# First attention layer: bank of the last first-score, place of the residual addition, and the order of the weight preparation

## The reference, cut to what matters

```python
x = _layernorm(x + attn0(x))   # 16 heads of 8, rotary positions, softmax(q k^T / sqrt(8)) v, then w_out and b_out
x = _layernorm(x + ffn0(x))    # ternary W_fc, gelu, layer norm with ln_w, ln_b, ternary W_proj
x = _layernorm(x + attn1(x))   # q = k, 16 heads mixed by W_x (16x16), then W_out
x = _layernorm(x + ffn1(x))    # silu(gate) * up, then down; int32 weights divided by 127
```

## Time and profile before

| | us |
|---|---|
| median of 3 runs | 1529.43 (1526.62 to 1534.0) |
| profiled run | 1530.18 |
| span from first to last instruction | 1527.9 |
| mean granted TensorE clock | 0.976 of full |
| TensorE busy / VectorE / ScalarE / GpSimd | 95% / 77% / 69% / 63% of the span |

### The profile page before, as it was taken

How to read it: one execution, slowest core, us unless ns; L and a number is a source line. 1 busy time by engine, 2 the same in 40 slices (tenths; PEclk the granted TensorE clock), 3 DMA queues, 4 the chain that set the end, 5 groups by cost and what they waited for, 6 DMA issues and landing times. The chain is left out here.

```text
span 1527.9 us, 55309 instructions
## 1 busy us (share of the span) xinstructions
PE 1456.4 (95%) x17642; PEld 1141.6 (75%) x17642; DVE 1180.8 (77%) x3338; ACT 1056.9 (69%) x2581; POOL 967.4 (63%) x1160
## 2 busy tenths in 40 slices
PE   5999999999999899979999999999999999998998
PEld 3445555554554499959989999999999999897997
DVE  4688888888888478878887888788878887864666
ACT  2477777777778888856777777777777777773332
POOL 4465565656554167777777877787778777852222
PEclk7699999999999999979999999999999999999999
DMA  5345454454444100122222222222222222201211
GB/s 146 105 128 135 132 140 128 132 140 126 134 131 135 34 32 33 55 74 79 82 69 90 76 79 69 90 76 80 69 90 76 80 70 85 75 23 32 65 62 52
DMA packets 174124, 133.93 MB, mean 88 GB/s; under 512 B 13787, under 2 KB 145126, under 8 KB 174054
## 3 DMA queue, kind: packets, MB, share of 16 engines
q1 hardware_dynamic: 172944, 132.37, 30.0%
q10 hardware_dynamic: 1110, 0.66, 0.1%
HBM read 64.82 MB, written 55.05 MB: 78 GB/s over the span
## 5 line engine op out<-in xcount | busy, mean ns | idle before, releaser
L971 DVE TENSOR_REDUCE shifts<-bank 128x2 bf16<-128x512 f32 x1024 | 682.2, 686 | 158.7 <-PE bank L1123 158.1
L912 ACT ACTIVATE probs<-bank 128x512 f32<-128x512 f32 x1024 | 579.9, 595 | 120.1 <-PE bank L1109 116.3
L1071 PE MATMUL bank<-values,probs 64*128 64x129 f32 x8192 | 577.8, 276 | 0.9 <-DVE o_even L938 0.7
L1071 PEld LDWEIGHTS bank<-values,probs 64*128 64x128 f32 x8192 | 528.8, 188 | 20.4 <-issue 4.5
L1123 PE MATMUL bank<-stack 48*128 48x256 bf16 x2048 | 373.3, 277 | 29.7 <-DVE shifts L971 24.1
L1109 PE MATMUL bank<-stack 49*128 49x256 bf16 x2048 | 373.3, 274 | 7.6 <-ACT probs L912 2.4
L715 POOL TENSOR_TENSOR values<-mix,v_in 128x1024 f32<-128x1024 f32 x128 | 302.3, 2363 | 0.0
L1109 PEld LDWEIGHTS bank<-stack 49*128 49x128 bf16 x2048 | 163.9, 95 | 139.4 <-ACT probs L912 89.7
L724 POOL TENSOR_TENSOR o_odd<-o_odd,scaled 128x256 f32<-128x256 f32 x224 | 163.5, 730 | 128.0 <-ACT scaled L838 124.3
L838 ACT ACTIVATE scaled<-bank,recips 128x128 f32<-128x128 f32 x448 | 138.6, 360 | 92.8 <-DVE recips L965 92.7
L1123 PEld LDWEIGHTS bank<-stack 48*128 48x128 bf16 x2048 | 156.2, 96 | 54.0 <-DVE shifts L971 37.8
(11 more groups left out here) (165 smaller groups left out, 2176.8 us busy)
## 6 DMA issues: line engine op xcount, KB each, us to landing
stack<-score_parts SPq DMA_DIRECT2D x64, 512.0 KB, 4.2
stack<-score_parts SPq DMA_DIRECT2D x256, 96.0 KB
score_parts<-parts SPq DMA_DIRECT2D x256, 64.0 KB, 2.1
score_parts<-parts SPq DMA_DIRECT2D x128, 96.0 KB, 2.6
score_parts<-parts SPq DMA_DIRECT2D x64, 192.0 KB, 2.3
x_in_f<-x_all SPq DMA_DIRECT2D x64, 128.0 KB, 2.0
score_parts<-parts SPq DMA_DIRECT2D x64, 128.0 KB, 2.2
x_in<-in_L_attn_x SPq DMA_DIRECT2D x32, 128.0 KB, 2.1
```

What stands on the lines that cost most here:

```text
L912: act.activation(probs[:, s % RING, :, :].rearrange("p t n -> p (t n)"), s2[s % 2][:, :], ACT.Exp, scale=scale).then_inc(exp_done, 1)
L971: dve.tensor_reduce(shifts[:, :, hf, col], s1_bank(s)[:, :].rearrange("p (t n) -> p t n", t=TILES), op=ALU.max, axis=AX.X, negate=True).th ...
L1071: return pe.matmul(pv_bank(h)[:, q * (D + 1):(q + 1) * (D + 1)], probs[rows, h % RING, t, q * P:(q + 1) * P], values[b.odd][rows, t, h, :] ...
```

## The change

Four things:

1. `s1_order` becomes banks 0, 1, 2 five times and then 1, so slot 14 uses bank 2 instead of 0. Slots 0 and 2 now wait for maxima four slots back, slot 14 for one three back; slots 15 and 1 still for one two back.
2. In the first attention the residual addition stands ahead of the maximum of slot 14.
3. In the preparation, the int weights are scaled and transposed (into banks 0, 1, 2) in `middle`, ahead of step -2; `mix` is copied by ScalarE in a new `middle` phase of its own; the ternary `W_fc` compare moves behind the scaling of `W_proj`; the small transposes go to banks 3 and 5, the sums to bank 4, `W_fc` to bank 5. TensorE waits for `mix` and the int weights ahead of step -1, and for the rest only ahead of step 0.
4. In step -2 the last three of the ten scratch writes of batch 0 are issued from ScalarE's queue instead of the sync engine's.

```diff
-COPIES = {"proj": 1, "mix": 1 + HD, "fc": 2 + HD, "ffn1": 5 + HD}
+COPIES = {"mix": HD, "ffn1": HD + 3, "proj": HD + 4, "fc": HD + 5}
...
+    @middle.engine("scalar")
+    def _(act):
+        act.wait_ge(small_turned, 1)
+        mixed = bank[5][:, 128:384].rearrange("p (g h) -> p h g", h=HEADS)
+        for d in range(HD):
+            act.activation(core.mix[:, :, :].rearrange("p h (g d) -> p h g d", d=HD)[:, :, :, d], mixed,
+                           ACT.Copy).then_inc(copied, 1)
+
     @late.engine("scalar")
     def _(act):
+        act.wait_ge(ffn1_turned, 1)
+        for k, to in enumerate((core.w1_gate, core.w1_up, core.w1_down)):
+            act.activation(to[:, :, :].rearrange("p c d -> p (c d)"), bank[k][:, 0:3 * D], ACT.Copy).then_inc(copied, 1)
         act.wait_ge(cols_ready, 1)
...
         dve.wait_ge(small_turned, 1)
-        dve.tensor_copy(core.cols[:, :], bank[1][:, 0:10]).then_inc(cols_ready, 1)
+        dve.tensor_copy(core.cols[:, :], bank[3][:, 0:10]).then_inc(cols_ready, 1)
+        dve.wait_ge(load_ffn1, 48)
+        dve.tensor_scalar(scaled[:, :, :, :].rearrange("p a c d -> p (a c d)"),
+                          raw_int[:, :, :, :].rearrange("p a c d -> p (a c d)"), float(np.float32(1.0 / 127.0)), None,
+                          ALU.mult).then_inc(scaled_ready, 1)
         dve.wait_ge(gamma_total, 1)
...
     @late.engine("vector")
     def _(dve):
-        dve.tensor_scalar(below[:, 0, :, :], raw_fc[:, :, :], bounds[:, 1, 0:1], None, ALU.is_lt).then_inc(below_ready, 1)
         dve.wait_ge(proj_turned, 1)
         dve.wait_ge(cols_ready, 1)
         for c in range(4):
             dve.tensor_scalar(scaled_proj[:, c, :], bank[3][:, c * D:(c + 1) * D], core.cols[:, c:c + 1], None,
                               ALU.mult).then_inc(proj_scaled, 1)
+        dve.tensor_scalar(below[:, 0, :, :], raw_fc[:, :, :], bounds[:, 1, 0:1], None, ALU.is_lt).then_inc(below_ready, 1)
         dve.wait_ge(below_ready, 2)
         ternary(dve, 0, raw_fc)
...
         pe.wait_ge(sums_ready, 2)
-        pe.matmul(bank[0][:, 0:2], ones[:, :], totals[:, :], start=True, stop=True).then_inc(gamma_total, 1)
+        pe.matmul(bank[4][:, 0:2], ones[:, :], totals[:, :], start=True, stop=True).then_inc(gamma_total, 1)
+        pe.wait_ge(scaled_ready, 1)
+        for k in range(3):
+            for c in range(3):
+                last = pe.transpose(bank[k][:, c * D:(c + 1) * D], scaled[:, k, c, :], core.ident[:, :])
+        last.then_inc(ffn1_turned, 1)
...
-    s1_order = (0, 1, 2) * 4 + (0, 1) * 2 if first else (0, 1) * 8
+    s1_order = (0, 1, 2) * 5 + (1,) if first else (0, 1) * 8
...
-                parts_out_in_stack_order(i.plus(2), MIDDLE, writes)
+                parts_out_in_stack_order(sp, i.plus(2), MIDDLE, FIRST_SHARE if starting else writes)
...
         def step(i, on):
             for s in range(HEADS):
+                if first and s == 0 and isinstance(i.half, int) and i.number() == -2:
+                    act.wait_ge(parts_ready, 1)
+                    parts_out_in_stack_order(act, i.plus(2), FIRST_SHARE, writes)
...
+                if first and s == slots.out and on(-1):
+                    add_residual(i)
                 if on(1):
                     max_of_head(i.plus(1), s)
...
-    final("tensor", late, late_taken=1, copied=COPIES["ffn1"])
+    final("tensor", middle, copied=COPIES["ffn1"])
     attn0.at(-1)
+
+    final("tensor", late, late_taken=1)
+    final("tensor", middle, copied=COPIES["fc"])
     final("tensor", attn0, ones_ready=4)
```

More of the change, by code:

```diff
@@ L297, in _ @@
         act.activation(turned_proj[:, :, :].rearrange("p c d -> p (c d)"), bank[3][:, :], ACT.Copy).then_inc(copied, 1)
[L298 to L301, removed]
         act.wait_ge(fc_turned, 1)
[L303 to L307, removed]
+        act.activation(core.w0_fc[:, :, :].rearrange("p c d -> p (c d)"), bank[5][:, :], ACT.Copy).then_inc(copied, 1)
     @early.engine("gpsimd")
@@ L431, in _ @@
         for c in range(4):
-            last = pe.matmul(bank[0][:, D:2 * D], shift_cols[:, c, :], turned_proj[:, c, :], start=(c == 0), stop=(c == 3))
+            last = pe.matmul(bank[4][:, 2 * D:3 * D], shift_cols[:, c, :], turned_proj[:, c, :], start=(c == 0), stop=(c == 3))
         last.then_inc(proj_summed, 1)
@@ L579, in stack_rows, with parts_out_in_stack_order @@
         return slice(parity * TILE_ROWS, parity * TILE_ROWS + rows)
+    def parts_out_in_stack_order(eng, b, lo, hi):
+        for k in range(lo, hi):
+            parity, k = divmod(k, 5)
+            split = parts[b.odd][parity * TILE_ROWS:(parity + 1) * TILE_ROWS, :, :, :]
+            if k == 4:
+                k_and_q = split.rearrange("p k e n -> p (k e) n")[:, 1:5:3, :]
+                eng.dma_start(scratch[b.odd, :, parity, USED - 1, :, :].rearrange("e r n -> r e n"), k_and_q).then_inc(parts_written, 16)
+                continue
+            s, m = RUNS[k // 2]
+            to = scratch[b.odd, :, parity, s:s + m, :, :].rearrange("e s r n -> e r s n")
+            if k % 2 == 0:
+                eng.dma_start(to[0], split[:, 0:m, 1, :]).then_inc(parts_written, 16)
+            else:
+                q = K_PART[s]
+                eng.dma_start(to[1], split[:, q:q + 1, 0, :].broadcast_to([TILE_ROWS, m, TOK])).then_inc(parts_written, 16)
     @phase.engine("sync")
@@ L965, in recip_head, with add_residual @@
             dve.reciprocal(recips[:, h % 2, :], sums).then_inc(recips_ready, 1)
+        def add_residual(i):
+            b = i.plus(-1)
+            wait(dve, x_ready, times(i, -3 if first else -2, n) * TILES)
+            if first:
+                dve.wait_ge(added_ready, times(i, -1, n))
+            dve.wait_ge(out_in_psum, times(i, -1, n))
+            dve.tensor_tensor(y_of(b)[:, :, :], m1[:, 0:TOK].rearrange("p (t d) -> p t d", t=TILES),
+                              core.x_all[:, b.number(), :, :], op=ALU.add).then_inc(y_ready, 1)
         def max_of_head(b, s):
```

69 lines of the change are left out of this document (19 added, 50 removed).

## The result

| | before | after |
|---|---|---|
| median, us | 1528.81 (4 runs, 1526.62 to 1534.0) | 1514.88 (4 runs, 1513.02 to 1516.91) |
| profiled run / span, us | 1530.18 / 1527.9 | 1516.91 / 1514.7 |
| mean granted TensorE clock | 0.976 | 0.984 |
| TensorE / VectorE / ScalarE / GpSimd busy | 95 / 77 / 69 / 63% | 96 / 78 / 70 / 64% |

The ratio of the medians is 0.9905, with a 95% interval of 0.9883 to 0.9926: the change saves 13.9 us, by the interval 11 to 18. The forecast was 12.1 us and 1517.3; the time lies inside the range of 1511.5 to 1526.

A forecast was written before the change was run, and what follows sets the result against it. The prediction took as bound a loop of TensorE up to slot 14, VectorE's four instructions and TensorE from slot 1. 8.9 us (step) plus 3.2 (start) off 1529.43 gave 1517.3 us, range 1511.5 to 1526.

The forecast's parts named there:

- The step: First attention: residual ahead of maximum 14 takes 0.33 us off each 14.86 us step, 27 times, 8.9 us.
- half microsecond of room: First attention, TensorE's slot 1: about 0.5 us of room left after the residual's move, nothing else becoming last there.
- room ahead of maximum 14: VectorE, first attention: 0.76 us idle in front of maximum 14, inside which the residual's 0.41 us would run.
- The banks: First scores, other bank order: zero in the steady steps; gives room only if slot 1's wait vanished.
- The order of the preparation: Start: mix and int weights sooner bring step -1 to about 33.2 from 37.17, 4.0 us sooner, bounds 2 and 5.
- The scaling beside GpSimd's L804: Preparation: VectorE's scaling, issued at 18.0, gets through only after GpSimd's instruction ends at 19.20, ending at 19.9.
- The price for L812: Preparation, GpSimd: the last part of batch 0's split is pushed from 19.28 by up to 0.6 us.
- The three writes: Start, ScalarE's queue: at most about 2 us sooner; without them the stack comes last at 34.8, taking 1.6 of 4.0.
- The survival of the start's gain: Start, low clock up to 68 us: of 4.0 us, 2.4 to 4.0 survive; 3.2 taken, the middle.
- Rival D: Clock rises before the work does, another 2 us, and the residual's whole 0.41 goes: 1512 us; chance 0.07.
- The sum: Whole kernel: 8.9 us from the steps and 3.2 from the start, 12.1 off 1529.43, giving 1517.3 us.

The follow-up runs named there:

- Residual alone: The kernel before with only the first attention's residual addition moved ahead of the maximum of slot 14; 1518.84 us, ratio 0.9941.
- the later rotation: The kernel after with the rotation of q behind the maximum of slot 15 instead of ahead of it; 1504.59 us, ratio 0.9844.
- residual twice: The kernel after with a second, equal residual addition, into a tile that nothing reads, directly ahead of the residual; 1515.62 us, ratio 0.9919.
- start alone: The kernel after with the old bank order and the residual behind the maximum again, keeping the new preparation and three writes; 1522.68 us, ratio 0.9961.
- Start filled: The kernel before with 23 more transposes of the identity, which nothing reads, at four places of the preparation; 1525.59 us, ratio 0.9981.
- banks alone: The kernel before with only slots 12 to 15 of the first scores in banks 0, 1, 2, 1; 1528.0 us, ratio 0.9995.
- the kernel after with the old banks: The kernel after with only the bank order line put back (0, 1, 0, 1 in slots 12 to 15); 1516.43 us, ratio 0.9919.
- all writes on sync: The kernel after with all ten scratch writes of batch 0 issued from the sync engine's queue again; 1515.94 us, ratio 0.9919.
- its old banks: The kernel after with the rotation of q behind the maximum of slot 15 and the old bank order; 1506.54 us, ratio 0.9863.
- the k projection first: The kernel after with q's rotation behind maximum 15 and, in slot 2, the k projection ahead of the values product; 1491.29 us, ratio 0.9751.

## Why the prediction came out right, point by point

**The step.** Right in place, mechanism and size. The forecast: steps of 14.52 us, idle time ahead of maximum 14 down to 0.3, the wait at slot 1 down to 0.36. The rows: 14.51, 0.43 and 0.36. Residual alone gave 9.4 us where 27 x 0.33 = 8.9 were written. Of the half microsecond of room that the prediction saw behind slot 1, the later rotation used another 0.33 before a new wait of 0.20 appeared; more was not tried. Of the room ahead of maximum 14, residual twice shows that it was larger than was needed.

**The banks.** Right: zero alone, zero in the kernel after, zero with slot 1's wait gone. The last case was left open by the prediction ("gives room only if"), and nothing was there.

**The order of the preparation.** The first score was to come 4.0 us sooner and came 4.77 in the kernel after and 5.11 in start alone. The steps in between, forecast and measured in the kernel after: end of the scaling 19.9 and 19.95; transposes until 22.1 and 22.18; rotation of k 24.2 and 23.93; last stack read landed at 32.8 at the latest and at 27.73 + 5.0 = 32.7, though the first score needs only the first read, which had landed at 31.4. `W_fc` was to be turned by 33.5 and was by 31.81 + 0.66 = 32.5. Most of this 1.0 us is the clock's, which the prediction had taken as low up to 68 us. The earlier trace rows show that only from 50 us on, and in the trace of the kernel before the clock was at 1.00 from 27.1 to 30.5 and from 40.7 to 44.2 us. In the kernel after it was at 1.00 from 28.3 to 38.5, so from the first L437 to the end of L445 it took 32.47 - 29.85 = 2.62 us. The same work took the kernel before 31.39 + 1.06 - 29.08 = 3.37:

```profile
29.08 1.16 PE L428 MATMUL bank<-scaled_proj,ones 128*128 128x128 f32 x8 [2.42 <-DVE scaled_proj L380]
```

In start alone L445 began at 30.50, 2.0 us ahead of the forecast, and the stack read came last. That the first score of the kernel after lies near the forecast is in part luck, then: with the start unchanged between them, seven profiles have it anywhere from 31.15 to 33.30. In the kernel after the scaling was issued 1.2 us later than forecast, since the projection ahead of it took 2.08 us and not 1.13. PE of the kernel before, and of the kernel after:

```profile
14.97 1.13 PE L1228 MATMUL bank<-x_t,w_qk 128*128 128x256 f32 x4 [0.47 <-ACT x_t L899]
```
```profile
15.22 2.08 PE L1238 MATMUL bank<-x_t,w_qk 128*128 128x256 f32 x4 [0.47 <-ACT x_t L905]
```

That is the duration of the low clock, as the earlier trace rows have it with 2.05 for the four products at 18.52 (the record of the granted clock begins only at 28.3 us in that profile). The `mix` copies, too, began at 18.58 and not near 17 (in start alone at 16.78), and in the waiting time of ScalarE all the same.

Two readings of this part are borne out by rows. The scaling beside GpSimd's L804 ended only behind it, as I had taken it from the earlier trace rows: in start alone, issued at 17.95, it ended at 19.77, against 19.9 by the prediction. In the kernel after it was issued between two of GpSimd's instructions and took 0.75 us; that it ended at 19.95 there, nearly as forecast, is luck. The price for L812 was bounded by 0.6 and is 1.70 - 1.16 = 0.54 in the kernel after and 0.40 in start alone. The Trainium skill's "GPSIMD Engine Reference" (Key points), which the prediction set against the move, agrees with these rows as far as it goes; whether the scaling is of the kinds that it names, no row shows.

The three writes were not right in mechanism, though the number fits. Without them the first score was to be at 34.8, held by the stack, and it was at 34.65, held by TensorE's own products at the low clock. The prediction counted with the landing of the second read, where the first score needs the first. By the estimate above the writes are worth 0.6 us there and not 1.6.

**The survival of the start's gain.** This is the term that I had named the weakest. The prediction: "I take 3.2, the middle" between 2.4 and 4.0. Start alone measured 5.5 us, 3.7 to 8.2, so it was put too small there. What failed is the assumption that both ends start from: that the clock's low stretch ends at the same time or moves with the work. In the profiled runs it did better than that. It ended at 68.0 us in the kernel before, at 55.6 in the kernel after, 51.5 in start alone. The work there was about 7 us ahead and the clock 12 to 17. The lead grows from 4.8 us at the first score to 6.9 at 65 us, while 4.0 was to shrink. Rival D had this mechanism ("The rise comes before the work does"), at a size of 2 us.

Start filled shows that this is a cause of its own. It leaves the first score where it was, only adds products ahead of it, and gains 2.4 us (1.5 to 4.3). So a preparation can pay twice: for the work that it moves ahead, and for keeping TensorE occupied while it would otherwise wait. How large the second share is in the kernel after can't be told from these runs. The low stretches also move with nothing changed at the start. With the old start they ended at 61.3 us in residual alone and at 68.0 and 68.3 in the kernel before and banks alone. With the new start they ended at 61.9 in the kernel after with the old banks, and between 50.9 and 56.5 in the seven other profiles. Over the 45 runs of the kernel before that stood beside the experiments the median of the 19 with a mean clock of 0.979 or less is 1529.99 us, that of the 10 with 0.984 or more 1527.64. The Trainium skill ("TensorE: Matmul & The Clock Gate", The HAM clock gate) says that such transitions move from run to run; the rows agree.

**The sum.** The parts alone give 9.4 + 5.5 + 0.2 = 15.1, all together 13.9, or 11.8 and 11.6 by the two kernels that differ from it by the old banks or by an addition that costs nothing. All of these agree within their intervals, and the forecast of 12.1 lies among them. So the 2.4 us by which the forecast missed the kernel after can't be given to a term. They are as large as the error of the start term by start alone, 5.5 - 3.2 = 2.3. But beside the residual's 9.4 the three kernels with both parts leave 4.5, 2.4 and 2.2 for the start, and 3.2 is in the middle of these.

**What stays open.** In the profiled runs of the kernel after and of start alone 4 to 5 us of lead go between 664 and 799 us. At the place there is a read of the second attention's stack that comes late. PE of the kernel before, and of the kernel after:

```profile
769.79 0.28 PE L1123 MATMUL bank<-stack 48*128 48x256 bf16 x1 [0.53 <-DMA stack<-score_parts]
```
```profile
755.32 0.39 PE L1133 MATMUL bank<-stack 48*128 48x256 bf16 x1 [2.73 <-DMA stack<-score_parts]
```

Behind it the clock of the kernel after is low for 3.4 us. The same read waits 2.64 us in start alone, 1.39 with all writes on sync, 0.55 with the old banks and 0.23 with the residual alone; with the later rotation it waits 1.70, with its old banks 2.38, with the k projection first 1.40. No part of the change touches this attention. Still, the lead lost between the 6000th and the 7800th product is 0.4 us or less in the three experiments with the old start and 0.5 to 5.2 in the eight kernels with the new one, so a connection with the start is not excluded. As to its weight: where most is lost, in start alone (5.2), the kernel after (4.1) and rotation later (3.9), the profiled run is the slowest of all runs of its kernel, 3.8, 2.0 and 3.5 us above the median. With the old banks and with all writes on sync 0.5 and 0.9 are lost, and the profiled run is 0.1 below and 0.8 above. So the medians seem to hold much less of this loss than the profiles do. I made no experiment on it.

## What to carry to other kernels

An engine that waits once in every step may be part of a loop of causes: walk back from the wait until an engine has an idle time in front of it, and what stands between that idle time and the wait and has its input earlier belongs ahead of the idle time. Here the first such instruction gave 9.4 us and the same walk on the new profile another 10, and the wait that then appeared led to an order worth 13: stop only when the wait is gone. Count the start of a kernel by its work and by its clock apart: here a preparation that left TensorE waiting was paid for after it as well, with 2.4 us by start filled. And where two things can hold an instruction, look in the trace which of them did: the first score without the three writes came within 0.15 us of its forecast for another reason.

## What the runs showed of the hardware that was not expected

- The order of three groups of products changed their time with no wait noted inside them: values (fp32), turned shifts (bf16), k projection (fp32) took 1.91 us to the next score, k projection, values, turned shifts 1.72 us.
- 23 transposes that nothing reads made a kernel faster: 1525.59 against 1527.95 us, with the stretch at a granted clock of 0.50 over by 55.2 us and not 68 in the one profile of each.
- VectorE's scaling of int32 to fp32 took 1.82 us when it was issued 0.06 us after GpSimd had begun an instruction of 1.27 us, and GpSimd's next took 1.56 and not 1.16. Issued at 19.20, between two of GpSimd's, it took 0.75, and GpSimd's next took 1.70. All eight profiles with the new start show one of these two pictures, within 0.02 us: two the first, six the second. So the scaling was lengthened only where GpSimd had begun first, and GpSimd's next instruction was longer in both.
- Three of ten scratch writes on a second queue brought the stack reads forward by 29.07 - 27.30 = 1.77 us, 0.59 for each write taken out of the sequence.
